# The inverse of the decay blocks kept as two 64x64 blocks per chunk in tiles of 64 columns, and turned two chunks at a time

## The chip, the cores and the metric

The kernel runs on one core of one Trainium2 chip, in float32 where nothing else is said. The metric is the device time of one execution in microseconds, the median of several runs. A core has TensorE (matmuls into PSUM; a transposition, here a "turn", is a matmul with the identity), VectorE, ScalarE and GpSimd (which read and write SBUF, the first two of them PSUM as well), and DMA queues. Each engine works through its own queue in order and waits on semaphores for the others.

## The reference, cut to what matters

Two layers: grouped attention with a mixture of experts behind it, then a gated delta rule with another mixture of experts. Only the gated delta rule is touched. It has 16 key heads, two value heads (units e = 0, 1) to each, 1024 tokens, and is, token by token:

```
S = S * exp(g_t)
kS = k_t . S
S = S + beta_t * k_t (x) (v_t - kS)
o_t = q_t . S
```

The kernel takes it in chunks of 128 tokens. Within a chunk the updates of all tokens come from one triangular system: with U the strictly lower triangular matrix of decayed products k.k times beta, what is wanted is P = (1 + U)^-1 (times beta), 128x128, for 8 chunks and 2 units of each key head.

## The kernel before

The last stage runs a loop over the 16 key heads (lines 1409, 1656, 1801, 2003: one loop on each engine). In each turn of the loop: the decays, k.k and q.k products, the inverse P, and then the scan over 8 chunks, which carries the state S (lines 1515 to 1547). The next head's projection (`project`, L1273), convolution (`conv_op`, L1860, L1862, L1871; written out as a list `todo` from which `more(n)` takes steps) and its copies are laid between the steps of the inverse and the scan, in a fixed order per engine.

The inverse. P is first made for the 16x16 blocks on the diagonal (VectorE, L2023 to L2038, all 16 matrices at once as 128x16 columns). Its last steps spread the blocks to full 128x128 matrices `decay_P` (`e_p`): unit 0 on VectorE (L2042), unit 1 on GpSimd (L1826). TensorE turns these 16 matrices (L1461, four PSUM banks), and ScalarE copies the turned ones to `gmask_Q` (`gm_q`, L1680), so Q = P^T. Then three doublings, level 4 (blocks of 16 to 32), level 5 (32 to 64) and the last (64 to 128). At each of levels 4 and 5, for each unit:

- X = U Q, on 64x64 tiles: low rows (LO, partitions 0 to 63) to low PSUM partitions and high (HI) to high, 16 matmuls of 64 columns (L1476); a float32 matmul is two MATMUL records in the trace, a turn is one
- VectorE takes X through a mask `lmask` into SBUF (L2061, 8 x 64 columns)
- Y = P X, the same tiles (L1486)
- VectorE subtracts Y from half of the columns of Q (L2067)
- TensorE turns Q, 8 matrices of 128x128 per unit, into four banks (L1493), and ScalarE copies them to `decay_P` (L1690).

The last doubling fills one corner of P only: X on one tile (L1500), a copy on 64 partitions (L2071), Y transposed on one tile (L1509), and a copy into the corner of `decay_P` (L1694). Between them stands the first `project_z` (L1321). GpSimd then makes the next head's `gmask_Q` (L1726, 128x2048), which waits for L1500. The scan reads all of `decay_P` (L1533) and begins S with L2094. It waits for both L1694 copies; L1520 is its first matmul that needs S.

In what follows e0 and e1 are the two units. VectorE's order in the doublings is: mask e0, `more(1)`, mask e1, Q e0, Q e1, `more(3)`.

## Time and profile before

| | |
|---|---|
| time, median of 3 runs | 2122.12 us (2114.63 to 2125.47) |
| the profiled execution's own time | 2117.74 us |
| its span | 2115.8 us |
| mean granted clock of TensorE | 0.976 |
| TensorE matmuls busy | 1917.6 us, 91% |
| TensorE weight loads busy | 1402.3 us, 66% |
| VectorE busy | 1505.7 us, 71% |
| ScalarE busy | 984.2 us, 47% |
| GpSimd busy | 759.0 us, 36% |
| DMA, mean | 53 GB/s |

A line number is that of the kernel before. Busy times of different engines overlap, and so do matmuls of one engine; what counts for the time is which engine the others wait for, stage by stage. A timeline row merges instructions of one line: its length runs from the first's start to the last's end, and the last matmul's end lies in the next row's time.

### The profile page before, as it was taken

The page shows a single profiled execution, that of the slowest core. Times are in us where ns is not written, and L with a number is a line of the kernel's source. Part 1 is how long each engine was busy: PE and PEld are TensorE (multiplying, and loading weights), DVE is VectorE, ACT ScalarE, POOL GpSimd, SP SyncE. Part 2 cuts the span into 40 slices and gives each one's busy share as a digit, 9 for nine tenths or more (in the row PEclk, how much of TensorE's full clock was granted, in tenths as well). Part 3 has the DMA queues.
Part 4 walks back from the last instruction along what each step waited for, and adds up shares of the span by engine and source line. Part 5 has one row for each costly group of instructions (what it writes and reads, how often), then busy time and mean ns, then how long its engine had stood idle before and what let it go on. Part 6 is the DMA issues. An engine that isn't in the chain of part 4 may idle for free.

```text
span 2115.8 us, 43478 instructions
## 1 busy us (share of the span) xinstructions
PE 1917.6 (91%) x15082; PEld 1402.3 (66%) x15082; DVE 1505.7 (71%) x2430; ACT 984.2 (47%) x2535; POOL 759.0 (36%) x685
## 2 busy tenths in 40 slices
PE   4578886888799999999999999999999999999998
PEld 3246662333555687877878778787687777877877
DVE  5786771111677687787787877878778787787887
ACT  1012224777213354645545455455564555645544
POOL 4730002110300334616336164362543624526343
PEclk9689998999899999999999999999999999999999
DMA  6635661000122200010010000100001001010010
GB/s 245 209 91 200 184 178 55 26 20 1 55 60 70 82 17 35 5 35 30 15 35 10 30 30 15 35 30 10 30 15 35 30 10 40 5 35 30 15 45 20
DMA packets 75254, 111.75 MB, mean 53 GB/s; under 512 B 23318, under 2 KB 56742, under 8 KB 72006
## 3 DMA queue, kind: packets, MB, share of 16 engines
q1 hardware_dynamic: 71694, 102.32, 15.1%
q0 software_dynamic: 3072, 8.39, 1.3%
q10 hardware_dynamic: 446, 0.48, 0.1%
q8 instruction: 26, 0.43, 0.1%
q14 instruction: 16, 0.13, 0.0%
HBM read 85.80 MB, written 28.52 MB: 54 GB/s over the span
## 4 chain that ended last, share of the span: by engine, by line
PE 51%; DVE 16%; issue 4%; ACT 3%; POOL 0%; DVEq 0%; ACTq 0%; POOLq 0%
PE ps L1273 5%; PE ps L1311 4%; PE ps L1321 4%; DVE conv L1862 3%; DVE P L2034 3%; DVE P_term L2031 3%; PE ps L1544 3%; PE ps L1493 3%; PE ps L1533 3%; PE ps L1428 3%; PE ps L1417 3%; PE ps L1546 3%; PE ps L1520 2%; PE ps L1450 2%; PE ps L1525 2%
## 5 line engine op out<-in xcount | busy, mean ns | idle before, releaser
L1862 DVE SCALAR_TENSOR_TENSOR conv<-raw,tap_st,conv 128x1024 f32<-128x1024 f32 x204 | 299.5, 1468 | 3.6
L1273 PE MATMUL ps<-xnT,w_conv_st 128*128 128x512 f32 x544 | 247.6, 599 | 0.0
L1842 POOL TENSOR_TENSOR o<-o,silu_z 128x256 f32<-128x256 f32 x128 | 138.5, 1082 | 255.5 <-DVE silu_z L1882 141.7
L816 DVE TENSOR_REDUCE m_part<-ps 128x1 f32<-128x640 f32 (+7 forms) x176 | 176.4, 1027 | 67.1 <-PE ps L667 53.5
L1726 POOL TENSOR_TENSOR gmask_Q<-upto,g 128x2048 f32<-128x2048 f32 x17 | 61.4, 3611 | 363.5 <-PE ps L1500 335.5
L998 ACT ACTIVATE probs<-ps 128x1024 f32<-128x1024 f32 (+7 forms) x256 | 145.9, 660 | 58.1 <-PE ps L933 28.7
L1273 PEld LDWEIGHTS ps<-xnT,w_conv_st 128*128 128x128 f32 x544 | 98.9, 191 | 101.1 <-issue 96.2
L1565 ACT COPY raw<-ps 128x512 f32<-128x512 f32 x136 | 80.7, 594 | 173.4 <-PE ps L1273 173.4
L1822 POOL TENSOR_TENSOR kq_decayed<-conv,decay_rows 128x1024 f32<-128x1024 f32 x64 | 159.3, 2521 | 0.0
L1321 PE MATMUL ps<-w_z_st,xnT 128*128 128x256 f32 x512 | 148.8, 393 | 0.0
L903 POOL DMA_INDIRECT slot_outputs<-scratch_slots_y,token_slots x32 | 30.6, 958 | 310.9 <-POOLq L496 202.0
L644 PE MATMUL ps<-k_stack,q_stack 128*128 128x512 bf16 (+3 forms) x384 | 101.6, 357 | 35.8 <-DVE m_part L816 17.8
L1025 DVE COPY oT<-ps 128x1024 f32<-128x1024 f32 x8 | 9.8, 1225 | 171.6 <-PE ps L920 171.6
L933 PE MATMUL ps<-q_stack,k_stack 128*128 x384 | 100.0, 335 | 33.6 <-ACT probs L998 24.4
L1311 PE MATMUL ps<-w_out_st,xn_nat 128*128 128x256 f32 x544 | 126.5, 386 | 3.3 <-ACT xn_nat L1598 2.5
L1311 PEld LDWEIGHTS ps<-w_out_st,xn_nat 128*128 128x128 f32 x544 | 101.8, 192 | 20.3 <-ACT xn_nat L1598 5.7
L1674 ACT ACTIVATE v_nat<-ps,norm_k 128x128 f32<-128x128 f32 x256 | 69.7, 383 | 96.1 <-PE ps L1291 96.1
L933 PEld LDWEIGHTS ps<-q_stack,k_stack 128*128 x384 | 35.9, 98 | 117.4 <-issue 86.8
L1826 POOL TENSOR_TENSOR decay_P<-P,block_mask 128x1024 f32<-128x1024 f32 x16 | 46.0, 2872 | 172.4 <-DVE P L2038 172.4
L2096 DVE SCALAR_TENSOR_TENSOR S<-S,unit_scalars,ps 128x128 f32<-128x128 f32 x192 | 58.1, 344 | 64.7 <-PE ps L1544 64.7
L1698 ACT COPY W<-ps 128x256 f32<-128x256 f32 x128 | 47.7, 373 | 114.6 <-PE ps L1533 112.5
L1571 ACT ACTIVATE tanh_conv<-conv 128x1024 f32<-128x1024 f32 x68 | 71.8, 1055 | 37.0 <-DVE conv L1862 35.0
(345 smaller groups left out, 4728.9 us busy)
## 6 DMA issues: line engine op xcount, KB each, us to landing
decay_rows<-scratch_egc SPq DMA_DIRECT2D x17, 1024.0 KB, 4.7
w_conv_st<-in_w_conv SPq DMA_DIRECT2D x17, 512.0 KB, 3.3
scratch_slots_x<-yacc SPq DMA_DIRECT2D x8, 1024.0 KB, 14.9
slot_rows<-scratch_slots_x SPq DMA_DIRECT2D x16, 512.0 KB, 4.7
scratch_slots_y<-slot_outputs SPq DMA_DIRECT2D x16, 512.0 KB, 3.4
w_gate_up<-in_gu SPq DMA_DIRECT2D x8, 768.0 KB
w_gate_up<-in_gu SPq DMA_DIRECT2D x32, 192.0 KB
kq_decayed<-in_gu SPq DMA_DIRECT2D x22, 256.0 KB, 2.8
```

The costliest lines, as they stand in the source:

```text
L644: return pe.matmul(ps[:, bank, at:at + hi - lo], m.qst[:, REP * i + h, qt * P:(qt + 1) * P], m.kst[:, i, lo:hi], start=first, stop=last)
L816: dve.tensor_reduce(dst, src, AX.X, ALU.max).then_inc(s_max, 1)
L933: mm = pe.matmul(ps[:, b0 + done // HALF, 0:w], m.kst[:, bass.ds(i, 1), kt * P:(kt + 1) * P], m.qst[:, bass.ds(i * REP + h, 1), kt * P + d ...
L998: nc.scalar.activation(pr[:, kt % 2, h, 0:cols], ps[:, 2 * (n % 3):2 * (n % 3) + 2, :].rearrange("p b n -> p (b n)")[:, 0:cols], ACT.Exp, ...
L1273: mm = pe.matmul(ps[:, 6 + n % 2, :], wc[:, k, (n // 2) * P:(n // 2 + 1) * P], m.xnT[:, k, (n % 2) * HALF:(n % 2 + 1) * HALF], start=k == ...
L1311: mm = pe.matmul(ps[:, n, (c % 2) * D:(c % 2 + 1) * D], oT[:, e, c * P:(c + 1) * P], wo[:, e, :], start=e == 0, stop=e == 1)
L1321: mm = pe.matmul(ps[:, 5, 0:256], m.xnT[:, k, c * P:(c + 1) * P], wz[:, k, :], start=k == 0, stop=k == KT - 1)
L1565: nc.scalar.copy(raw[:, n // 2, at:at + HALF], ps[:, 6 + n % 2, :]).then_inc(s_raw, 1)
L1571: nc.scalar.activation(thc[:], cv[:, t, :], ACT.Tanh).then_inc(s_tc, 1)
L1822: g.tensor_tensor(kqe[:, e, a, :], cv[:, a, :], egr[:, e, :], ALU.mult).then_inc(s_kqe, 1)
L1842: g.tensor_tensor(oc, oc, zs[:, c, :], ALU.mult).then_inc(s_oz, 1)
L1862: op = dve.scalar_tensor_tensor(out=cv[:, t, :], in0=raw[:, t, at:at + T], scalar=tap[:, t, at:at + 1], in1=cv[:, t, :], op0=ALU.mult, op1 ...
```

## The change

P and Q of levels 4 and 5 are block diagonal in two 64x64 blocks per chunk. They are now held as 64 columns per chunk instead of 128: `qd` and `pd`, each 128 partitions x 2 units x 8 chunks x 64 columns, both in the room of `gmask_Q`. Consequences:

- The spreads write half (128x512): a mask of half the blocks, `bmask4`.
- All three turns take two chunks at once, [128 x 2*64], so 4 turns per unit instead of 8, into one bank (2 + e). A turn puts chunk 2j on partitions 0 to 63 and chunk 2j+1 on 64 to 127, its low block in columns 0 to 63 and its high block in 64 to 127.
- After the first turn, ScalarE puts the halves back in their places with four copies per unit on 64 partitions (4 chunks x 64 columns each). After the turn of level 4 there is one plain copy (128x512): P stays in the turned layout, and the X and Y matmuls of level 5 take it from there, so that they use all four 64x64 tiles: X goes from rows h to the columns of the chunk's parity, Y back from these rows to h. X and Y there lie in two banks per unit. After the turn of level 5 there are four copies on 64 partitions per unit, straight to the diagonal blocks of `decay_P`.
- X and Y stream 32 columns per block, not 64; VectorE's mask and subtraction are 128x256.
- `lmask` is made for two levels instead of seven; two small reductions of constants are added before the loop.

Core of the diff:

```diff
+        bmask4 = sb("block_mask_of_half", [P, NB // 2])
+        lmask = sb("lmask_of_half", [P, 2, P // 4])
+        xs32 = xs[:, :, 0:NC // 2, :].rearrange("p e c (q n) -> p e (c q) n", q=2)
+        gm_room = gm_q[:].rearrange("p e c n -> p (e c n)")
+        qd = gm_room[:, 0:NC * P].rearrange("p (e c n) -> p e c n", e=2, c=NC)
+        pd = gm_room[:, NC * P:].rearrange("p (e c n) -> p e c n", e=2, c=NC)
+        def place(lv, c, h):
+            j, hi = c // 2, int(h is HI)
+            if lv == FIRST:
+                return h, c, 0, c, 0, c
+            return (LO, HI)[c % 2], 2 * j + hi, hi, j, c % 2, j
+        def halves(e):
+            turned = ps[:, 2 + e, :].rearrange("p (j h n) -> p j h n", h=2, n=64)
+            return [(h, odd, turned[(LO, HI)[odd], :, int(h is HI), :]) for h in (HI, LO) for odd in range(2)]
+        def base(lv, e):
+            return (e, (4, 0)[e], (4, 1)[e])[lv - FIRST]
 tensor:
-                    for c in range(NC):
-                        mm = pe.transpose(ps[:, 2 * e + c // 4, (c % 4) * P:(c % 4 + 1) * P], e_p[:, e, c, :], m.ident[:])
+                    for j in range(NC // 2):
+                        mm = pe.transpose(ps[:, 2 + e, j * P:(j + 1) * P], pd[:, e, 2 * j:2 * j + 2, :].rearrange("p c n -> p (c n)"), m.ident[:])
...
-                                dst = ps[h, e, c * 64:(c + 1) * 64].rearrange("p (b s) -> p b s", s=s)
-                                mm = pe.matmul(dst, ua[h, e, c, 1, h], gm_q[h, e, c, :].rearrange("p (b t s) -> p b t s", t=2, s=s)[:, :, 0, :],
+                                g, at, bank, slot, _, _ = place(lv, c, h)
+                                dst = ps[g, bank + base(lv, e), slot * 32:(slot + 1) * 32].rearrange("p (b s) -> p b s", s=s)
+                                mm = pe.matmul(dst, ua[h, e, c, 1, h], qd[h, e, c, :].rearrange("p (b t s) -> p b t s", t=2, s=s)[:, :, 0, :],
                                                start=True, stop=True)
...
-                                mm = pe.matmul(ps[h, e, c * 64:(c + 1) * 64], e_p[h, e, c, h], xs[h, e, c, :], start=True, stop=True)
+                                g, at, _, _, bank, slot = place(lv, c, h)
+                                mm = pe.matmul(ps[h, bank + base(lv, e), slot * 32:(slot + 1) * 32], pd[g, e, at, :], xs32[g, e, at, :], start=True, stop=True)
...
-                        for c in range(NC):
-                            mm = pe.transpose(ps[:, 2 + 2 * e + c // 4, (c % 4) * P:(c % 4 + 1) * P], gm_q[:, e, c, :], m.ident[:])
+                        for j in range(NC // 2):
+                            mm = pe.transpose(ps[:, 2 + e, j * P:(j + 1) * P], qd[:, e, 2 * j:2 * j + 2, :].rearrange("p c n -> p (c n)"), m.ident[:])
 scalar:
-                    nc.scalar.copy(chunks(gm_q[:, e]), two_banks(2 * e)).then_inc(s_q, 1)
+                    for h, odd, src in halves(e):
+                        last = nc.scalar.copy(qd[h, e, odd::2, :], src)
+                    last.then_inc(s_q, 1)
...
-                    nc.scalar.copy(chunks(e_p[:, e]), two_banks(2 + 2 * e)).then_inc(s_pt, 1)
+                    if lv == FIRST:
+                        nc.scalar.copy(chunks(pd[:, e]), ps[:, 2 + e, :]).then_inc(s_pt, 1)
+                    else:
+                        for h, odd, src in halves(e):
+                            last = nc.scalar.copy(e_p[h, e, odd::2, h], src)
+                        last.then_inc(s_pt, 1)
 gpsimd and vector (spread; the same on pc[:, 0:NC] for unit 0):
-                g.tensor_tensor(e_p[:, 1].rearrange("p c (b i) -> p c b i", i=BLK),
-                                pc[:, NC:, :].unsqueeze(2).broadcast_to([P, NC, NB, BLK]),
-                                bmask[:].unsqueeze(1).unsqueeze(3).broadcast_to([P, NC, NB, BLK]), ALU.mult).then_inc(s_p1, 1)
+                g.tensor_tensor(pd[:, 1].rearrange("p c (b i) -> p c b i", i=BLK),
+                                pc[:, NC:, :].unsqueeze(2).broadcast_to([P, NC, NB // 2, BLK]),
+                                bmask4[:].unsqueeze(1).unsqueeze(3).broadcast_to([P, NC, NB // 2, BLK]), ALU.mult).then_inc(s_p1, 1)
 vector:
-                        mask = m.lmask[:, lv, :].unsqueeze(1).broadcast_to([P, NC, 64])
-                        dve.tensor_tensor(xs[:, e], ps[:, e, :].rearrange("p (c n) -> p c n", c=NC), mask, ALU.mult).then_inc(s_xt, 1)
+                        mask = lmask[:, lv - FIRST, :].unsqueeze(1).broadcast_to([P, NC, 32])
+                        if lv == FIRST:
+                            made, taken = ps[:, e, 0:NC * 32].rearrange("p (c n) -> p c n", c=NC), xs32[:, e]
...
+                        dve.tensor_tensor(taken, made, mask, ALU.mult).then_inc(s_xt, 1)
...
-                        dst = gm_q[:, e, :, :].rearrange("p c (b t s) -> p c b t s", t=2, s=s)[:, :, :, 0, :]
-                        dve.tensor_tensor(dst, dst, ps[:, e, :].rearrange("p (c b s) -> p c b s", c=NC, s=s), ALU.subtract).then_inc(s_yt, 1)
+                            dst = qd[:, e].rearrange("p c (b t s) -> p c b t s", t=2, s=s)[:, :, :, 0, :]
+                            made = ps[:, e, 0:NC * 32].rearrange("p (c b s) -> p c b s", c=NC, s=s)
...
+                        dve.tensor_tensor(dst, dst, made, ALU.subtract).then_inc(s_yt, 1)
```

## Rows read from the trace of the kernel before

**Rows 1.** The page: the chain that ended last, its share of the span by engine.
```profile
PE 51%; DVE 16%; issue 4%; ACT 3%; POOL 0%; DVEq 0%; ACTq 0%; POOLq 0%
```

**Rows 2.** Windows, one turn of the head loop: busy time (instructions) per engine, granted clock.
```profile
1368.50:1455.40 86.90, 83.63 (x722) 66.50 (x720) 70.36 (x118) 46.23 (x132) 38.56 (x32) 1.00 0.07 24
```

**Rows 3.** Source view, line 2042 (duration min/median/max, first and last start).
```profile
L2042 DVE TENSOR_TENSOR decay_P<-P,block_mask x16: 1224/1224/1224, 738.4 to 2041.6; 128x1024 f32<-128x1024 f32 x16
```

**Rows 4.** Timeline of TensorE, one head: start, us, line, tiles, matmuls, idle time before.
```profile
1426.18 8.75 PE L1273 MATMUL ps<-xnT,w_conv_st 128*128 128x512 f32 x20
1435.05 1.09 PE L1461 MATMUL ps<-ident,decay_P 128*128 128x128 f32 x8
...
1440.38 2.08 PE L1476 MATMUL ps<-gmask_Q,att_U 64*64 64x64 f32 x64
1442.42 1.15 PE L1486 MATMUL ps<-X,decay_P 64*64 64x64 f32 x32
1443.89 1.15 PE L1486 MATMUL ps<-X,decay_P 64*64 64x64 f32 x32 [0.33 <-DVE X L2061]
1444.97 1.98 PE L1273 MATMUL ps<-xnT,w_conv_st 128*128 128x512 f32 x4
1446.79 1.91 PE L1493 MATMUL ps<-ident,gmask_Q 128*128 128x128 f32 x16
1448.63 2.08 PE L1476 MATMUL ps<-gmask_Q,att_U 64*64 64x64 f32 x64
...
1452.46 1.15 PE L1486 MATMUL ps<-X,decay_P 64*64 64x64 f32 x32 [0.65 <-DVE X L2061]
...
1455.43 2.08 PE L1500 MATMUL ps<-gmask_Q,att_U 64*64 64x64 f32 x32
...
1458.50 2.08 PE L1509 MATMUL ps<-decay_P,X 64*64 64x64 f32 x32
...
1461.43 0.61 PE L1533 MATMUL ps<-v_nat,decay_P 128*128 128x128 f32 x4
...
1463.97 0.71 PE L1520 MATMUL ps<-S,kq_decayed 128*128 128x128 f32 x4 [0.17 <-DVE S L2094]
```

**Rows 5.** Timeline of VectorE, the same stretch.
```profile
1434.91 2.42 DVE L1860 TENSOR_SCALAR conv<-raw,tap_st 128x1024 f32<-128x1024 f32 x1
...
1441.58 0.69 DVE L2061 TENSOR_TENSOR X<-ps,lmask 128x512 f32<-128x512 f32 x1 [0.29 <-PE ps L1476]
1442.19 0.74 DVE L1860 TENSOR_SCALAR conv<-raw,tap_st 128x1024 f32<-128x1024 f32 x1
...
1445.08 0.69 DVE L2067 TENSOR_TENSOR gmask_Q<-gmask_Q,ps 128x512 f32<-128x512 f32 x1 [0.74 <-PE ps L1486]
...
1446.82 2.60 DVE L1862 SCALAR_TENSOR_TENSOR conv<-raw,tap_st,conv 128x1024 f32<-128x1024 f32 x2
...
1457.57 1.30 DVE L2071 COPY X<-ps 64x512 f32<-64x512 f32 x2
...
1459.44 4.28 DVE L1862 SCALAR_TENSOR_TENSOR conv<-raw,tap_st,conv 128x1024 f32<-128x1024 f32 x2
...
1464.37 0.41 DVE L1882 SCALAR_TENSOR_TENSOR silu_z<-tanh_z,ps 128x256 f32<-128x256 f32 x1
```

**Rows 6.** Source view, line 446 (both shapes, first and last start).
```profile
L446 PE MATMUL ps<-w_attn_sb,xnT x64: 248/276/323, 37.1 to 44.1; 128*128 128x64 f32 x32, 128*128 128x32 f32 x32
```

**Rows 7.** Windows, line 920 alone: busy us (matmuls).
```profile
335.60:337.70 2.10, 1.92 (x16) 0.42 (x16) 1.00 0.41 111
```

**Rows 8.** Timeline of GpSimd, the same stretch.
```profile
1433.91 2.87 POOL L1826 TENSOR_TENSOR decay_P<-P,block_mask 128x1024 f32<-128x1024 f32 x1 [10.56 <-DVE P L2038]
1457.71 3.61 POOL L1726 TENSOR_TENSOR gmask_Q<-upto,g 128x2048 f32<-128x2048 f32 x1 [20.93 <-PE ps L1500]
```

**Rows 9.** Groups by line and shape, ScalarE (busy us, mean ns, idle before).
```profile
L1698 ACT COPY W<-ps 128x256 f32<-128x256 f32 x128 | 47.7, 373 | 114.6 <-PE ps L1533 112.5
...
L1680 ACT COPY gmask_Q<-ps 128x1024 f32<-128x1024 f32 x32 | 32.4, 1012 | 13.0 <-PE ps L1461 13.0
```

More of the change, by code:

```diff
@@ L165, in build @@
         m.future = sb("future", [P, P], BF16)
-        m.lmask = sb("lmask", [P, LEVELS, P // 2])
+        m.lmask = sb("lmask", [P, 2, P // 2])
         m.minus_half = sb("minus_half", [P, 1])
@@ L619, in _ @@
             step.link(g.memset(m.lmask[:], 1.0))
-            for lv in range(LEVELS):
-                s = 1 << lv
-                ap = m.lmask[:, lv, :].rearrange("p (b s) -> p b s", s=s)
+            for n in range(2):
+                s = 1 << (FIRST + n)
+                ap = m.lmask[:, n, :].rearrange("p (b s) -> p b s", s=s)
                 step.link(g.affine_select(out=ap, in_=ap, compare_op=ALU.is_ge, fill=0.0, base=-s,
@@ L1499, in _ @@
                     for c in range(NC):
-                        mm = pe.matmul(ps[HI, e, c * 64:(c + 1) * 64], ua[LO, e, c, 1, HI], gm_q[LO, e, c, LO], start=True, stop=True)
+                        mm = pe.matmul(ps[HI, base(LEVELS - 1, e), c * 64:(c + 1) * 64], ua[LO, e, c, 1, HI], qd[LO, e, c, :], start=True, stop=True)
                     mm.then_inc(s_x, 1)
@@ L1508, in _ @@
                     for c in range(NC):
-                        mm = pe.matmul(ps[LO, e, c * 64:(c + 1) * 64], xs[HI, e, c, :], e_p[HI, e, c, HI], start=True, stop=True)
+                        mm = pe.matmul(ps[LO, base(LEVELS - 1, e), c * 64:(c + 1) * 64], xs[HI, e, c, :], e_p[HI, e, c, HI], start=True, stop=True)
                     mm.then_inc(s_y, 1)
@@ L1693, in _ @@
                     act.wait_ge(s_y, i * ND + NT + e + 1)
-                    nc.scalar.activation(e_p[LO, e, :, HI], ps[LO, e, :].rearrange("p (c n) -> p c n", c=NC), ACT.Copy,
+                    nc.scalar.activation(e_p[LO, e, :, HI], ps[LO, base(LEVELS - 1, e), :].rearrange("p (c n) -> p c n", c=NC), ACT.Copy,
                                          scale=-1.0).then_inc(s_pt, 1)
@@ L1798, in _ @@
             g.tensor_copy(tap[:], m.taps[:, 1]).then_inc(s_taps, 1)
-            pool.wait_ge(s_dve, 5)
+            pool.wait_ge(s_dve, 7)
             passed()
@@ L1991, in _ @@
                     step(dve.tensor_reduce(hmask[:], bmask[:].rearrange("p (q t) -> p t q", t=2), AX.X, ALU.add))
+                    step(dve.tensor_reduce(bmask4[:], bmask[:].rearrange("p (h b) -> p b h", h=2), AX.X, ALU.add))
+                    step(dve.tensor_tensor(lmask[:], m.lmask[:, :, 0:P // 4], m.lmask[:, :, P // 4:], ALU.add))
                     step.wait()
@@ L2041, in _ @@
                 dve.wait_ge(s_ch, i * SUBS + n)
-                dve.tensor_tensor(e_p[:, 0].rearrange("p c (b i) -> p c b i", i=BLK),
-                                  pc[:, 0:NC, :].unsqueeze(2).broadcast_to([P, NC, NB, BLK]),
-                                  bmask[:].unsqueeze(1).unsqueeze(3).broadcast_to([P, NC, NB, BLK]), ALU.mult).then_inc(s_p0, 1)
+                dve.tensor_tensor(pd[:, 0].rearrange("p c (b i) -> p c b i", i=BLK),
+                                  pc[:, 0:NC, :].unsqueeze(2).broadcast_to([P, NC, NB // 2, BLK]),
+                                  bmask4[:].unsqueeze(1).unsqueeze(3).broadcast_to([P, NC, NB // 2, BLK]), ALU.mult).then_inc(s_p0, 1)
                 todo = ([(0, k) for k in range(TAPS)] + [(1, 0), (0, TAPS)] + [(1, k) for k in range(1, TAPS)]
@@ L2059, in _ @@
                         dve.wait_ge(s_x, i * ND + n0 + e + 1)
-                        mask = m.lmask[:, lv, :].unsqueeze(1).broadcast_to([P, NC, 64])
-                        dve.tensor_tensor(xs[:, e], ps[:, e, :].rearrange("p (c n) -> p c n", c=NC), mask, ALU.mult).then_inc(s_xt, 1)
+                        mask = lmask[:, lv - FIRST, :].unsqueeze(1).broadcast_to([P, NC, 32])
+                        if lv == FIRST:
+                            made, taken = ps[:, e, 0:NC * 32].rearrange("p (c n) -> p c n", c=NC), xs32[:, e]
+                        else:
+                            made = ps[:, base(lv, e):base(lv, e) + 2, 0:NC * 16].rearrange("p b (j n) -> p b j n", n=32)
+                            taken = xs32[:, e].rearrange("p (j b) n -> p b j n", b=2)
+                            mask = lmask[:, lv - FIRST, :].unsqueeze(1).unsqueeze(1).broadcast_to([P, 2, NC // 2, 32])
+                        dve.tensor_tensor(taken, made, mask, ALU.mult).then_inc(s_xt, 1)
                         if e == 0:
@@ L2065, in _ @@
                         dve.wait_ge(s_y, i * ND + n0 + e + 1)
-                        dst = gm_q[:, e, :, :].rearrange("p c (b t s) -> p c b t s", t=2, s=s)[:, :, :, 0, :]
-                        dve.tensor_tensor(dst, dst, ps[:, e, :].rearrange("p (c b s) -> p c b s", c=NC, s=s), ALU.subtract).then_inc(s_yt, 1)
+                        if lv == FIRST:
+                            dst = qd[:, e].rearrange("p c (b t s) -> p c b t s", t=2, s=s)[:, :, :, 0, :]
+                            made = ps[:, e, 0:NC * 32].rearrange("p (c b s) -> p c b s", c=NC, s=s)
+                        else:
+                            dst = qd[:, e, :, 0:s].rearrange("p (j b) n -> p b j n", b=2)
+                            made = ps[:, base(lv, e):base(lv, e) + 2, 0:NC * 16].rearrange("p b (j n) -> p b j n", n=s)
+                        dve.tensor_tensor(dst, dst, made, ALU.subtract).then_inc(s_yt, 1)
                     more(3)
@@ L2070, in _ @@
                     dve.wait_ge(s_x, i * ND + NT + e + 1)
-                    dve.tensor_copy(xs[HI, e], ps[HI, e, :].rearrange("p (c n) -> p c n", c=NC)).then_inc(s_xt, 1)
+                    dve.tensor_copy(xs[HI, e], ps[HI, base(LEVELS - 1, e), :].rearrange("p (c n) -> p c n", c=NC)).then_inc(s_xt, 1)
                 silu_z(i, 0)
@@ L2114, in mix_out @@
                 dve.tensor_tensor(y[:, pair], y[:, pair], mixed[n % 2], ALU.add).then_inc(s_mixed, 1)
-            step.n = 5
+            step.n = 7
             early, late = slice(0, NC // 2), slice(NC // 2, NC)
```

## The prediction, on record before the changed kernel ran

> **What bounds the kernel now.** The page first: the chain that ended last runs over TensorE for 51% of the span, over VectorE for 16% and over ScalarE for 3% [rows 1]. Then one turn of the loop over the 16 key heads, between equal points of two turns: TensorE works 83.6 of 86.9 us at a granted clock of 1.00, VectorE 70.4, ScalarE 46.2, GpSimd 38.6 [rows 2]. The spread of P opens the part that is changed; its 16 starts lie from 738.4 to 2041.6 us, so a turn takes 1303.2 / 15 = 86.9 us [rows 3], and what one turn gains counts 16 times. Last, the timelines of one turn. The reader is to see in TensorE's [rows 4] that the doublings (1435.05 to 1461.43) are nearly gapless: only 0.33 us of idle time on VectorE before a Y at level 4, 0.65 us in the same place at level 5. So matmul time taken out there is won, until VectorE's queue comes up behind it; VectorE carries convolution steps between the pieces of the inverse [rows 5].
>
> **Turns.** 8 matmuls fewer in the first turn and 8 in each of the two others, 24 per key head. 16 of them take 1446.79 to 1448.63, 0.115 us each [rows 4]: 0.92 us for 8, 2.76 us in all, all on TensorE's path.
>
> **X and Y of levels 4 and 5.** They stream 32 columns, not 64, with the same 64-column weights. Would that be faster? Line 446 holds 32 matmuls of 64 and 32 of 32 columns with 128-column weights; its 64 starts go from 37.1 to 44.1, 0.111 us each whatever the columns, against 0.115 us for 128 columns above [rows 4, 6]. So with 128-column weights the weights set the pace below 128 columns. For 64-column weights the nearest row is the last X, one tile at a time with 64 columns: 32 in 2.01 us, 63 ns each, about half of 0.115 [rows 4]. I read that as the pace of the weights too and take no gain from the narrower stream. The lower bound of the cost is half.
>
> **Tiles of level 5.** Level 4 keeps its two tiles (low rows to low columns, high to high), which run side by side: 64 in 2.04 us, 32 ns each, half of the 63 ns of one tile [rows 4]. At level 5 all four tiles are used in turn. Line 920 tells that column tiles on the same rows overlap: 16 matmuls of 512 columns in 1.92 us, where one 512-column matmul of a projection takes 1.82 / 4 = 0.46 [rows 4, 7]. So four tiles will not be slower than two; whether they are faster is left open. I take 32 ns, with 15 (four side by side) and 63 (one at a time) as bounds.
>
> In the Trainium skill, "TensorE: Matmul & The Clock Gate", section "The mechanism", weight loads overlap running matmuls only between different row groups; the new Y of level 5 uses each row group twice in a row and would suffer. The trace disagrees: the last X stays in one row group and still issues every 63 ns. By the rule, Y would fall back to about one tile at a time, which the third rival below prices from rows.
>
> **VectorE.** The 128x512 operations on X and Q (0.69) become 128x256 (0.41, the silu_z row) [rows 5]: 0.28 less, eight times, of which only those ahead of a waiting Y or turn count. The spread of P falls from 1.22 to 0.69. GpSimd's own spread took 2.87 and ended at 1436.78; the convolution step that began at 1434.91 ended at 1437.33, right behind it, against 0.75 for such a step unhindered (1442.19, between two X masks) [rows 5, 8]. Half the elements end GpSimd's at about 1435.4, so VectorE's chain of four steps is through near 1440.0, not 1441.3, just before X needs it.
>
> **ScalarE.** The first copy (128x1024, 1.01) becomes four of 64x256. A 128x256 copy is 0.37 [rows 9], so four take at most 1.5; as copies in a row overlap somewhat, I take 1.2 for four and 2.3 for eight, against 1.9 for the two long copies. The level-4 copy falls to 0.59; the level-5 ones grow to 2.3 for both. Cover: in the first turn the projections (1.8 each) lie above it; behind level 5, 2.0 us of last X. With 1.5 for four the first X would still wait for TensorE alone, and L1509 would come 0.2 later. Without the cover the cost would be about 0.4 us per head and turn.
>
> **The sum, piece by piece.** Up to the first X: TensorE ends its fifth projection near 1434.8 (the row ends at 1434.93, and the next line's matmuls begin about 0.15 before a row's end, as 1446.79 does before 1446.95) and waits until 1435.05 for VectorE's spread [rows 4]; that 0.25 goes, and 0.92 of turns. First X at 1439.2, not 1440.38: 1.17 us won. ScalarE's last copy ends near 1438.8 and does not hold it.
> From the first X (now 0), before and after [rows 4, 5]: Y of the second head starts at 3.51, after at 2.98 (VectorE's mask is 0.3 shorter, then TensorE itself is the limit). Projection 1.82 and 8 turns: X of level 5 at 8.25, after 6.83. Here VectorE takes over: behind the second Q of level 4 it has three convolution steps (1445.08 to 1449.42 with that Q, so 3.7 for the steps). That Q now begins at 4.15 (Y at 2.98, 0.93 of matmuls, 0.24 until VectorE starts) and takes 0.35, so VectorE reaches the level-5 mask at 8.25, though X is ready at 8.05. Then mask 0.4, one convolution step 1.2, mask 0.4: second Y at 12.08, after 10.32. Turns: last X at 15.05, after 12.55; the second turn waits 0.2 for VectorE's Q. Then VectorE again: Q at 11.5 (10.32 + 0.93 + 0.24), then three steps (1.2 + 0.75 + 1.3), so the copy of X begins at 15.15 (17.19 before), and L1509 at 16.0 instead of 18.12. The scan begins at 18.93 instead of 21.05.
> One more late thing: the first S of the scan. gmask (3.61) starts behind the last X and ended at 1461.32; the two convolution steps begun at 1459.44 took 4.28 instead of 2.6 and ended at 1463.72, 2.4 behind gmask, and S came behind them, so L1520 waited 0.17 [rows 4, 5, 8]. After: gmask from 14.8 or 15.15 (a convolution step is running at its start) to 18.4 to 18.8, S's copies from 20.8 to 21.1 on. TensorE would be there at 21.3. L1520 at 23.59, after about 21.4: 2.2 won.
> In "SBUF — State Buffer", section "Who interferes with whom", the Trainium skill has a VectorE instruction with two SBUF inputs and a GpSimd one that reads SBUF exclude each other, whoever starts first; the two rows above agree, and by it gmask starts at 15.15. The sum is the same for either start.
> In all 1.17 + 2.18 = 3.35 us per head, 53.6 for 16. Of 5.2 us (2.8 of turns, 2.2 of VectorE's eight operations, 0.25) that is two thirds; the rest is swallowed where VectorE's queue sets the pace. Behind L1520 scan, outputs and the next head are unchanged and shift as a whole. The two more constants of VectorE and ten fewer mask instructions of GpSimd lie before the loop, under 0.5 us. The profiled execution took 2117.7 us (span 2115.8 and 1.9 around it), 4.4 below the median of the runs shown; 2117.7 - 53.6 = 2064, by the median 2068.5. I forecast 2066, halfway, and count the rivals from the same base (2119.6).
>
> **Rivals.**
> 1. Four tiles overlap, or the narrow streams count. If level 5 goes at 15 ns, X there is hidden by VectorE, and only the last Y shortens (0.47): 3.8 us per head, 2059. If level 4 goes so too, X, Y and VectorE's whole queue move up: replayed, 4.8 us, 2043. For: line 920. Against: line 446 has the weights as the pace. 0.22 together (0.07 for 2043).
> 2. Small waits that I left out (semaphores between more instructions, drains where tile shapes change, 0.14 behind each Y today): 0.3 to 1 us per head, 2071 to 2082. 0.17.
> 3. Row neighbours of Y at level 5 don't overlap: 64 matmuls at up to 63 ns; the first is partly under the mask wait, the second adds 0.9, about 1.35 in all: 2.0 us per head, 2088. Against: [rows 7]. 0.04.
> 4. No change to speak of: all of level 5 one tile at a time. 128 matmuls times 31 ns is 4 us, 0.8 of it under VectorE: 3.2 lost against 3.35 won: 2117. 0.03.
> 5. Slower: as 4, and every change of tile drains. From matmuls of one shape to another the path pays 0.14 (second Y of level 4, 0.93 of work, begins 1443.89; the projection 1444.97) [rows 4]. At 64 changes times 0.05 to 0.14 us: 3 to 9 us per head, 2165 to 2260. It decides from 3.35 / 64 = 52 ns per change with 2 or more tiles, or from 2 ns if the tiles don't overlap either. Against: line 920 changes its tile at each matmul without such a cost. 0.04.
> The forecast itself has 0.50, its own range 2060 to 2071.
>
> **Range and chances.** Leaving out 2043 below and the serial cases above, 2046 to 2084 holds a good 8 in 10. A measurement of this kernel (2114.6 to 2125.5) tells about 0.5%, 10.6 us, from no change. Faster: all but rivals 4 and 5, 0.93; same 0.03; slower 0.04.
>
> **What would show it.** Right: a turn of 83.5 us; L1493 with 256 matmuls, L1461 with 128; L1476 and L1486 with 32 columns and still 2.04 us per 64 at level 4; idle time of TensorE behind VectorE's X at level 5 grown from 0.65 to between 0.5 and 1; the POOL spread under 1.6; L1520 waiting little for S. Wrong: level 4's 64 matmuls in about 1 us (rival 1), level 5's at 4 us (rivals 4, 5), TensorE idle behind a ScalarE copy before the first X, or a clock below 1.00 in the loop.

## The result, and the profile after

The changed kernel takes 2143.63 us (median of 5 runs, 2136.76 to 2147.95), the kernel before 2122.12 on the same chip: 1.010 times the time before, 95% interval 1.008 to 1.013. So it is slower by 1%, where 2066 and a gain were forecast. The profiled execution took 2139.09 us, span 2137.2. (The runs further on were made on several chips, on which the kernel before takes 2087, 2084 and 2122 us; each is compared with the kernel before on its own chip, with a 95% interval in brackets.) A ratio leaves out runs that took over 1.5% longer than the fastest run of the same kernel, which concerns fill_narrow alone.

From the page of the kernel after: the span, the busy times, the granted clock in 40 slices, and the chain that ended last by engine.

```profile
span 2137.2 us, 42854 instructions
PE 1918.4 (90%) x14658; PEld 1407.5 (66%) x14698; DVE 1441.4 (67%) x2432; ACT 998.5 (47%) x2727; POOL 731.9 (34%) x675
...
PEclk9699998999799989989889898899988989889998
...
PE 58%; DVE 8%; ACT 6%; issue 2%; POOL 0%; DVEq 0%; ACTq 0%; POOLq 0%
```

The same clock line of the kernel before:

```profile
PEclk9689998999899999999999999999999999999999
```

The head loop fills the slices from about the 14th on. Before, every slice there was a 9; after, there are 8s all through the loop. VectorE's share of the chain fell from 16% to 8% and TensorE's rose from 51% to 58% [rows 1].

Windows of the kernel after, each one head (from one spread of P to the next); columns as in [rows 2]: length, busy time of PE, PEld, DVE, ACT and POOL, granted clock, DMA share, GB/s.

```profile
831.00:914.30 83.30, 78.85 (x698) 62.04 (x697) 66.38 (x117) 47.07 (x143) 37.13 (x33) 1.00 0.07 25
914.30:1003.10 88.80, 84.82 (x698) 67.54 (x697) 66.15 (x117) 47.07 (x143) 37.12 (x33) 0.92 0.06 24
...
1358.30:1448.80 90.50, 86.51 (x698) 68.95 (x697) 66.27 (x117) 47.05 (x143) 37.17 (x33) 0.91 0.07 23
```

These are the same 698 records with three lengths. Three of the 15 head windows look like the first, about 83.35 us; twelve have a clock below 1.00. Nine of those take about 88.8 us, two 90.5, and the loop's first 91.5. Before, a head took 86.9 at 1.00 [rows 2, 3]. Now one fallen head next to an undisturbed one, cut at the points where their work is the same: from the first X to the end of the last Y of level 5, then up to the scan.

```profile
836.50:847.40 10.90, 9.09 (x268) 7.65 (x268) 8.60 (x13) 4.04 (x6) 0.00 (x0) 1.00 0.15 48
847.40:856.40 9.00, 8.50 (x99) 7.43 (x93) 8.33 (x9) 4.89 (x13) 3.67 (x1) 1.00 0.00 0
919.80:930.70 10.90, 9.09 (x268) 7.68 (x268) 8.65 (x13) 4.04 (x6) 0.00 (x0) 1.00 0.13 48
930.70:944.40 13.70, 13.70 (x98) 12.26 (x92) 8.53 (x9) 4.56 (x12) 3.61 (x1) 0.50 0.00 0
```

The doublings are equal to the tenth. Right behind them the granted clock is 0.50, 1.2 instead of 2.4 GHz, for 13.7 us, and about a hundred records (98 and 99) take 13.7 us, not 9.0. It is so in each of the twelve: the clock is 1.00 in the first 15 us of the head and 0.50 to 0.52 from 16.7 to 30 us. The windows hold less TensorE work than they look: 9.09 us busy in 10.9.

TensorE's timeline of the undisturbed head, from the first X to the scan (start, us, line, tiles, records, idle time before):

```profile
836.42 2.06 PE L1500 MATMUL ps<-gmask_Q,att_U 64*64 64x32 f32 x64 [0.19 <-ACT gmask_Q L1706]
838.28 2.20 PE L1511 MATMUL ps<-X,gmask_Q 64*64 64x32 f32 x64
...
843.20 1.14 PE L1500 MATMUL ps<-gmask_Q,att_U 64*64 64x32 f32 x64
845.29 0.67 PE L1511 MATMUL ps<-X,gmask_Q 64*64 64x32 f32 x32 [0.95 <-DVE X L2101]
846.82 0.67 PE L1511 MATMUL ps<-X,gmask_Q 64*64 64x32 f32 x32 [0.86 <-DVE X L2101]
847.42 1.26 PE L1518 MATMUL ps<-ident,gmask_Q 128*128 128x128 f32 x8
848.61 2.08 PE L1525 MATMUL ps<-gmask_Q,att_U 64*64 64x64 f32 x32
851.18 1.13 PE L1344 MATMUL ps<-w_z_st,xnT 128*128 128x256 f32 x4 [0.50 <-ACT decay_P L1721]
852.24 2.08 PE L1534 MATMUL ps<-decay_P,X 64*64 64x64 f32 x32
...
855.18 0.61 PE L1558 MATMUL ps<-v_nat,decay_P 128*128 128x128 f32 x4
...
857.38 0.61 PE L1545 MATMUL ps<-S,kq_decayed 128*128 128x128 f32 x4
```

And of the fallen head, the part behind its second Y of level 5:

```profile
930.76 1.97 PE L1518 MATMUL ps<-ident,gmask_Q 128*128 128x128 f32 x8
932.66 3.67 PE L1525 MATMUL ps<-gmask_Q,att_U 64*64 64x64 f32 x32
...
938.26 3.67 PE L1534 MATMUL ps<-decay_P,X 64*64 64x64 f32 x32
...
943.63 0.96 PE L1558 MATMUL ps<-v_nat,decay_P 128*128 128x128 f32 x4
```

From the turn behind the last Y of level 5 to the scan it is 7.76 us in the one (847.42 to 855.18) and 12.87 in the other (930.76 to 943.63). No wait stands behind that: each line has the same records, each taking 1.6 to 1.8 times as long. These 5.1 us and 0.35 more in the first rows of the scan are the 5.5 that the head is longer.

ScalarE's copies of the halves, undisturbed head (the second row is all eight of level 5):

```profile
834.78 1.50 ACT L1706 COPY gmask_Q<-ps 64x256 f32<-64x256 f32 x4
...
848.11 3.02 ACT L1721 COPY decay_P<-ps 64x256 f32<-64x256 f32 x8 [0.68 <-PE ps L1518]
```

**The account.** Fifteen heads now take 1321.7 us, before 1303.2 [rows 3]. Without falls they would take about 1251.1, which is what the run fill_first below shows (mean 83.4; the loop's first head is 0.9 longer in it). So 52.1 us are won, and 70.6 given back in twelve heads, 5.9 each. The 16th head falls too (2.0 us over its time before), and 0.9 is lost ahead of the loop: 18.5 + 2.0 + 0.9 = 21.4, the whole difference of the spans, 2137.2 against 2115.8.

### The profile page after: what moved, and what is told of

The parts are those of the page before. It is cut to its first block, busy times and chain, and to the rows that moved or that the text cites. A ratio compares the mean times of both kernels' runs of the same rounds, so it can differ in the third digit from the quotient of the medians.

```text
span 2137.2 us, 42854 instructions
## 1 busy us (share of the span) xinstructions
PE 1918.4 (90%) x14658; PEld 1407.5 (66%) x14698; DVE 1441.4 (67%) x2432; ACT 998.5 (47%) x2727; POOL 731.9 (34%) x675
## 4 chain that ended last, share of the span: by engine, by line
PE 58%; DVE 8%; ACT 6%; issue 2%; POOL 0%; DVEq 0%; ACTq 0%; POOLq 0%
PE ps L1296 7%; PE ps L1344 5%; PE ps L1334 4%; PE ps L1473 3%; PE ps L1569 3%; PE ps L1558 3%; PE ps L1571 3%; DVE conv L1894 3%; PE ps L1440 3%; PE ps L1451 3%; PE ps L1534 2%; PE ps L1545 2%; ACT gmask_Q L1706 2%; PE ps L1525 2%; PE ps L1511 2%
## 5 line engine op out<-in xcount | busy, mean ns | idle before, releaser
L1894 DVE SCALAR_TENSOR_TENSOR conv<-raw,tap_st,conv 128x1024 f32<-128x1024 f32 x204 | 285.8, 1401 | 3.6
L1344 PE MATMUL ps<-w_z_st,xnT 128*128 128x256 f32 x512 | 165.3, 429 | 1.5 <-ACT decay_P L1721 1.5
L644 PE MATMUL ps<-k_stack,q_stack 128*128 128x512 bf16 (+3 forms) x360 | 94.7, 350 | 41.9 <-DVE m_part L816 21.1
L1344 PEld LDWEIGHTS ps<-w_z_st,xnT 128*128 128x128 f32 x512 | 90.3, 207 | 14.5 <-ACT decay_P L1721 1.9
```

Of the source, the lines that this page charges most:

```text
L644: return pe.matmul(ps[:, bank, at:at + hi - lo], m.qst[:, REP * i + h, qt * P:(qt + 1) * P], m.kst[:, i, lo:hi], start=first, stop=last)
L1344: mm = pe.matmul(ps[:, 5, 0:256], m.xnT[:, k, c * P:(c + 1) * P], wz[:, k, :], start=k == 0, stop=k == KT - 1)
L1894: op = dve.scalar_tensor_tensor(out=cv[:, t, :], in0=raw[:, t, at:at + T], scalar=tap[:, t, at:at + 1], in1=cv[:, t, :], op0=ALU.mult, op1 ...
```

## The experiments

The theory: the change does what was worked out, but TensorE has less to do in the doublings, and its clock falls behind them. The rival explanations: the fall comes from something else in the heads (other work, another execution), the four tiles do it, or the new tiles and copies cost time themselves. "Falls" are head windows with a granted clock below 1.00, out of 15, in the profiled execution; the head times are in us. The last three kernels leave products or turns out, as told at each, and are there for their times alone.

| kernel | ratio to before | falls | head, undisturbed | head, fallen |
|---|---|---|---|---|
| after | 1.010 [1.008, 1.013] | 12 | 83.35 | 88.8, 90.5 |
| after_again | 1.010 [1.007, 1.013] | 12 | 83.4 | 88.8, 90.5 |
| fill_gaps | 0.974 [0.971, 0.976] | 0 | 83.5 | |
| fill_first | 0.974 [0.972, 0.977] | 0 | 83.35 | |
| fill_no_wait | 0.974 [0.972, 0.975] | 0 | 83.3 | |
| turn_twice | 0.977 [0.974, 0.981] | 0 | 83.9 | |
| fill_narrow | 0.986 [0.981, 0.990] | 10 | 83.4 | 88.8, 90.5 |
| fill_elsewhere | 1.004 [1.002, 1.006] | 4 | 85.7 | 91.3 |
| wide_x | 1.006 [1.005, 1.008] | 11 | 83.4 | 88.9, 90.5 |
| two_tiles | 1.014 [1.011, 1.018] | 13 | 83.6 | 89.1, 90.7 |
| before_half_turns | 0.995 [0.993, 0.997] | 0 | 86.2 | |
| before_narrow4 | 1.008 [1.006, 1.010] | 8 | 86.8 | 88.5, 90.0 |
| before_narrow | 1.013 [1.007, 1.019] | 15 | | 88.3, 90.0 |

### fill_gaps: a matmul in each of the two waits of level 5

One matmul of 128x512 whose result nobody reads (two records), ahead of each wait for X at level 5. All else is the changed kernel.

```diff
 for e in range(2):
+    if lv > FIRST:
+        pe.wait_ge(s_raw, (i + 1) * 8 + 7)
+        for _ in range(1):
+            pe.matmul(ps[:, 6, :], m.ident[:], m.xnT[:, 0, 0:HALF], start=True, stop=True)
     pe.wait_ge(s_xt, i * ND + n0 + e + 1)
```

> The changed kernel, with one 128x512 matmul (identity on xnT, result thrown away, a PSUM bank nobody reads) ahead of each of the two waits for X at level 5, where TensorE was idle for 0.95 and 0.86 us. The clock theory (TensorE does too little in the doublings and is set to 1.2 GHz behind them) expects the clock to stay at 1.00 in all or most heads, a head of 83.4 to 84 us and about 2066 us in all. The rival (the fall belongs to the new form of levels 4 and 5, not to the idle time) expects heads of 88.8 us as now and 2140 to 2150 us.

Measured: 2032.08 against 2086.98, ratio 0.974. A head window, and TensorE's timeline at level 5:

```profile
790.50:874.00 83.50, 80.84 (x702) 62.59 (x701) 66.40 (x117) 47.09 (x144) 37.20 (x32) 1.00 0.07 25
```

```profile
803.09 1.14 PE L1500 MATMUL ps<-gmask_Q,att_U 64*64 64x32 f32 x64
804.15 1.13 PE L1507 MATMUL ps<-xnT,ident 128*128 128x512 f32 x2
805.21 0.67 PE L1515 MATMUL ps<-X,gmask_Q 64*64 64x32 f32 x32
805.81 1.12 PE L1507 MATMUL ps<-xnT,ident 128*128 128x512 f32 x2
806.86 0.67 PE L1515 MATMUL ps<-X,gmask_Q 64*64 64x32 f32 x32
```

The filler takes 1.06 us, about what the wait was (0.95 and 0.86), so the doublings end 0.15 later. All 15 heads are at 1.00. Two matmuls per head that compute nothing take the ratio from 1.010 to 0.974: the fall is the whole loss, and the rest of the change is worth 54.9 us. (0.974 of 2122.12 is 2066, as expected.)

### wide_x: X streams 64 columns again

X of levels 4 and 5 takes all 64 columns of Q, and VectorE picks the 32 that count.

```diff
-dst = ps[g, bank + base(lv, e), slot * 32:(slot + 1) * 32].rearrange("p (b s) -> p b s", s=s)
-mm = pe.matmul(dst, ua[h, e, c, 1, h], qd[h, e, c, :].rearrange("p (b t s) -> p b t s", t=2, s=s)[:, :, 0, :],
+mm = pe.matmul(ps[g, bank + base(lv, e), slot * 64:(slot + 1) * 64], ua[h, e, c, 1, h], qd[h, e, c, :],
                start=True, stop=True)
```

> The changed kernel with X of levels 4 and 5 streaming all 64 columns again instead of 32; the mask takes the 32 it needs. If 64-column weights set the pace, the time of X at level 4 stays at 2.04 us per 64 matmuls and TensorE moves twice the columns in it. Theory one (narrow streams at level 4 lower the activity) expects fewer falls of the clock, 2070 to 2110 us. Theory two (the idle time and four tiles at level 5 do it) expects 13 falls of 16 as now, 2140 us.

Measured: 2100.2, ratio 1.006. X at level 4 and at level 5:

```profile
1406.98 2.08 PE L1499 MATMUL ps<-gmask_Q,att_U 64*64 64x64 f32 x64 [0.20 <-ACT gmask_Q L1705]
...
1413.79 1.16 PE L1499 MATMUL ps<-gmask_Q,att_U 64*64 64x64 f32 x64
```

Twice the columns take the same time, 1.89 (to the first Y) against 1.86 for level 4 and 1.16 against 1.14 for level 5: the narrow stream wins nothing on TensorE. Eleven heads of 15 fall, one of them only to 0.98 (84.4 us). So the columns of X alone don't restore the clock.

### two_tiles: level 5 on two tiles at a time

```diff
-for c in range(NC):
+for c in (range(NC) if lv == FIRST else (0, 2, 4, 6, 1, 3, 5, 7)):
```

(for X and for Y; even chunks use two of the four tiles, odd chunks the other two)

> The changed kernel with level 5 in another order, all even chunks and then all odd ones, so that only two of the four tiles can run side by side. X and Y of level 5 should go back from about 1.1 to 2.0 us per 64 matmuls, in the place of the idle time; a head grows by the last Y alone, 0.5 us, 83.9. If idle time of TensorE at level 5 brings the clock down, it stays up now: about 2075 us. If the columns moved count and not the time in which something runs, nothing is gained: 2140 to 2155 us.

Measured: 2117.61, ratio 1.014.

```profile
1428.90 1.46 PE L1500 MATMUL ps<-gmask_Q,att_U 64*64 64x32 f32 x64
1430.99 0.92 PE L1511 MATMUL ps<-X,gmask_Q 64*64 64x32 f32 x32 [0.63 <-DVE X L2101]
1432.52 0.92 PE L1511 MATMUL ps<-X,gmask_Q 64*64 64x32 f32 x32 [0.60 <-DVE X L2101]
```

Less overlap (0.92 for a Y, not 0.67) fills part of the waits: 0.63 and 0.60 of idle time, not 0.95 and 0.86. Yet 13 heads fall. So the fall doesn't need four tiles at once, and a third less idle time doesn't help when it is narrow matmuls that fill it. The expectation of 2.0 us for 64 matmuls was too high: X took 1.46. For a Y both tiles have the same rows, and its 32 records still take 0.85 us (1432.52 to 1433.37), 27 ns each, against 63 for one tile.

### turn_twice: the turns of levels 4 and 5 made twice

```diff
-for j in range(NC // 2):
+for j in (*range(NC // 2), *range(NC // 2)):
```

> The changed kernel with every turn of levels 4 and 5 made twice in a row (8 matmuls per unit as before the change, the second set writing the same values). Costs TensorE 1.84 us per head, some of it under VectorE. The clock theory expects a clock at 1.00 and a head of 84.7 to 85.2 us, 2087 to 2096 us in all. If the taken-out turns have no part in it, 88.8 + 1.8 us per head, 2170 us.

Measured: 2039.02, ratio 0.977, no fall in 15 heads.

```profile
789.50:873.40 83.90, 80.43 (x714) 63.88 (x713) 66.57 (x117) 47.31 (x144) 37.14 (x32) 1.00 0.07 25
```

```profile
1475.42 0.67 PE L1511 MATMUL ps<-X,gmask_Q 64*64 64x32 f32 x32 [0.17 <-DVE X L2101]
1476.95 0.67 PE L1511 MATMUL ps<-X,gmask_Q 64*64 64x32 f32 x32 [0.86 <-DVE X L2101]
```

16 more turns a head (x714) cost 0.5 us of it and save the clock. They put back as many turns as the change had removed there. But they don't leave the waits as they were: the doubled turns of level 4 lie ahead of X, and the first wait of level 5 shrinks from 0.95 to 0.17, while the second stays at 0.86. So this run doesn't tell whether it is the turns themselves that help or the shorter wait. It does show that the second wait need not be filled.

### after_again, fill_narrow, fill_elsewhere, before_narrow

after_again is the changed kernel once more, beside the other three.

> The changed kernel itself, as a mark for the chip and the day. Both theories: 1.01 times the kernel before, heads of 83.35 us without and 88.8 to 90.5 with a fall of the clock, 12 to 14 falls in 16 heads.

Measured: 2105.7 against 2083.74, ratio 1.010, 12 falls. The falls are no accident of one execution or of one chip.

fill_narrow fills the two waits with eight matmuls of 64x64 weights and 32 columns, all on one tile:

```diff
+    if lv > FIRST:
+        pe.wait_ge(s_raw, (i + 1) * 8 + 7)
+        pe.sem_inc(s_passed, 1)
+        for _ in range(8):
+            pe.matmul(ps[LO, 6, 0:32], m.ident[LO, LO], m.xnT[LO, 0, 0:32], start=True, stop=True)
```

> As fill_gaps, but each gap is filled with 8 matmuls of 64x64 weights and 32 columns on one tile instead of one of 128x512: about the same time (16 records of 58 ns, 0.93 us), a small part of the array and few columns. If it counts that TensorE has something running, the clock stays up and the ratio to the kernel before is 0.974 again. If it counts how much of the array is moved, 12 to 14 falls and a ratio of about 1.01.

Measured: four runs of 2048.19, 2057.97, 2086.66 and 2094.74, with a mean granted clock of 0.973, 0.966, 0.952 and 0.947 (after_again on the same chip: 0.941). The ratio 0.986 is of the first two; the median of all four, 2072.32, is 0.994. The profile is of the run of 2086.66:

```profile
1319.02 1.09 PE L1508 MATMUL ps<-xnT,ident 64*64 64x32 f32 x16
1320.15 0.67 PE L1516 MATMUL ps<-X,gmask_Q 64*64 64x32 f32 x32
1320.61 1.09 PE L1508 MATMUL ps<-xnT,ident 64*64 64x32 f32 x16
1321.68 0.83 PE L1516 MATMUL ps<-X,gmask_Q 64*64 64x32 f32 x32
1322.44 1.97 PE L1523 MATMUL ps<-ident,gmask_Q 128*128 128x128 f32 x8
```

TensorE is busy without a gap through level 5, and the clock is at 1.2 GHz from the second Y on all the same (the turns behind it take 1.97, in an undisturbed head 1.26). Having TensorE busy in both waits is not enough, then: eight small matmuls take as long as one of 512 columns, and 10 heads fell in this execution. By their times and clocks the two shorter runs had fewer: above 0.974 of the kernel before, at 5.9 us a fall, the four times make about 3, 5, 10 and 11 falls (an estimate, from these times and the 70.6 us in twelve heads). One kernel can fall often in one execution and seldom in the next.

fill_elsewhere puts the two wide fillers ahead of the k.k products, a dense place:

```diff
 pe.wait_ge(s_acc, i * 16 + 16)
+for _ in range(2):
+    pe.matmul(ps[:, 6, :], m.ident[:], m.xnT[:, 0, 0:HALF], start=True, stop=True)
```

> The two filling matmuls of fill_gaps, but at the start of each head, ahead of the products of k with k, where TensorE is dense anyway; there they cost their full 1.75 us. If the place counts (the thin stretch of the doublings), 12 to 14 falls stay and a head takes 90.6 us on average or so, a ratio of 1.02 to 1.03. If only the work per head counts, the clock stays up: 85.1 us per head, a ratio of 0.985.

Measured: 2091.35, ratio 1.004.

```profile
792.50:883.80 91.30, 86.72 (x701) 68.23 (x700) 65.23 (x117) 46.83 (x143) 36.91 (x32) 0.93 0.07 23
883.80:969.50 85.70, 80.63 (x701) 62.81 (x700) 65.60 (x117) 46.81 (x143) 36.99 (x33) 1.00 0.08 24
```

An undisturbed head is 2.3 us longer, a little more than the two fillers (2.1). The falls go from 12 to 4, not to 0 and not 12 again. It fits neither "any extra work helps" nor "only work at the thin place helps"; the length of a head, which this edit changes too, may decide how often the fall is hit. That was not taken apart.

before_narrow is the kernel before with 32-column streams for X and Y of levels 4 and 5, its tiles and turns as they were. It leaves out the products of the other 32 columns, and VectorE takes what older products left in their place:

```diff
-dst = ps[h, e, c * 64:(c + 1) * 64].rearrange("p (b s) -> p b s", s=s)
-mm = pe.matmul(dst, ua[h, e, c, 1, h], gm_q[h, e, c, :].rearrange("p (b t s) -> p b t s", t=2, s=s)[:, :, 0, :],
+at = c * 64 + 32 * int(h is HI)
+dst = ps[h, e, at:at + 32].rearrange("p (b s) -> p b s", s=s)
+mm = pe.matmul(dst, ua[h, e, c, 1, h], gm_q[h, e, c, h].rearrange("p (b t s) -> p b t s", t=2, s=s)[:, :, 0, :],
...
-mm = pe.matmul(ps[h, e, c * 64:(c + 1) * 64], e_p[h, e, c, h], xs[h, e, c, :], start=True, stop=True)
+at = 32 * int(h is HI)
+mm = pe.matmul(ps[h, e, c * 64 + at:c * 64 + at + 32], e_p[h, e, c, h], xs[h, e, c, at:at + 32], start=True, stop=True)
```

> The kernel before with X and Y of levels 4 and 5 streaming 32 columns instead of 64 (the half on each block's own diagonal; VectorE still takes 64, so what stands in the other half of Q is left over from older products). Nothing else is changed. If 64-column weights set the pace, a head takes 86.8 us as before. If the narrow stream alone were enough to bring the clock down, 5 us per head more, a ratio of 1.03 to 1.04; I expect 0 to 4 falls, since the turns are all there, and a ratio of 1.00 to 1.01.

Measured: 2113.47, ratio 1.013.

```profile
895.24 3.78 PE L1273 MATMUL ps<-xnT,w_conv_st 128*128 128x512 f32 x4
...
1423.13 2.06 PE L1477 MATMUL ps<-gmask_Q,att_U 64*64 64x32 f32 x64
...
1426.61 1.12 PE L1488 MATMUL ps<-X,decay_P 64*64 64x32 f32 x32 [0.35 <-DVE X L2063]
...
1429.48 1.91 PE L1495 MATMUL ps<-ident,gmask_Q 128*128 128x128 f32 x16
...
1435.12 1.12 PE L1488 MATMUL ps<-X,decay_P 64*64 64x32 f32 x32 [0.67 <-DVE X L2063]
1436.18 3.63 PE L1495 MATMUL ps<-ident,gmask_Q 128*128 128x128 f32 x16
```

This is the cleanest of the runs. Times and waits of the doublings are those of [rows 4] (X 2.06 against 2.08, Y 1.12 against 1.15, idle 0.35 and 0.67 against 0.33 and 0.65), only the streams are narrower, and every one of the 15 heads falls, where 0 to 4 were expected. Eleven fall behind the Ys of level 5: the turns of 1436.18 take 3.63, those of 1429.48 took 1.91. The four heads of 90.0 us fall behind the Ys of level 4 already: the projection of 895.24 takes 3.78, in [rows 4] 1.98. The falls are short here, and a head costs 88.3 or 90.0 in place of 86.9. The narrow streams make the kernel 1.3% slower. (The values differ too, since half of them are left over from older products. That isn't taken apart here; before_half_turns below also works on left-over values and falls nowhere.)

### fill_first, fill_no_wait, before_half_turns, before_narrow4

fill_first keeps only the first of the two fillers (`if lv > FIRST and e == 0`).

> fill_gaps with the first of the two filling matmuls alone (half the dose). The density theory (what counts is how thin TensorE's work is over the stretch of level 4 and 5 as a whole) expects fewer falls than 13, between 0 and 6 of 16, a ratio of 0.974 to 0.99. If both gaps must be closed, 12 to 14 falls and 1.01.

Measured: 2068.93 against 2121.86, ratio 0.974, no falls, 83.35 a head. One matmul of 512 columns is enough. It fills the first wait; the second, 0.82 us in this run, stays.

fill_no_wait is fill_gaps without the wait ahead of the first `project_z`, for ScalarE's last copy of P. (Each last Y keeps its own wait for the copy that it reads.)

```diff
-pe.wait_ge(s_pt, i * ND + NT)
 project_z(i, 0)
```

> fill_gaps without the wait of project_z for ScalarE's level-5 copies, which the changed kernel's own banks no longer need and for which TensorE stood 0.5 us in each head. The clock stays at 1.00; a head of 83.0 to 83.3 us instead of 83.53, a ratio to the kernel before of 0.968 to 0.973. If VectorE's copy of X is what holds the next matmuls, nothing is gained: 0.974.

Measured: 2065.59, ratio 0.974, a head of 83.3 for 83.5.

```profile
848.33 2.05 PE L1537 MATMUL ps<-decay_P,X 64*64 64x64 f32 x32 [0.31 <-DVE X L2119]
```

The 0.50 of ScalarE's copies is gone, but 0.31 comes back one instruction later behind VectorE's copy of X. Too small to show in the ratio.

before_half_turns is the kernel before with only the even chunks turned at levels 4 and 5 (`for c in range(0, NC, 2)`); for the odd chunks an older P is left.

> The kernel before with only the even chunks turned at levels 4 and 5 (4 matmuls per unit instead of 8; the odd chunks of P are left over). X and Y keep 64 columns. A head is 1.4 to 1.8 us shorter if the clock holds, 85.0 to 85.4, a ratio of 0.98. If fewer turns alone make the stretch thin enough, falls of the clock take that back: a ratio of 1.00 to 1.03. From before_narrow I expect the narrow streams to be the greater part and 0 to 3 falls here.

Measured: 2111.13, ratio 0.995, no falls, 86.2 a head (86.9 before).

```profile
1361.12 1.15 PE L1486 MATMUL ps<-X,decay_P 64*64 64x64 f32 x32 [0.54 <-DVE X L2061]
```

16 turns less are 1.84 us of TensorE [rows 4], of which 0.7 is won. The rest goes into new waits for VectorE, 0.54 ahead of the first Y of level 5, 0.20 in the turns behind it and 0.30 ahead of L1509. With half of the turns, and with waits of 0.54 and 0.65 at level 5, but with 64-column streams, no head falls. So neither fewer turns nor waits of that length bring the clock down by themselves.

before_narrow4 is before_narrow with the narrow streams at level 4 only.

> before_narrow with the narrow streams at level 4 alone, which stands between two projections; level 5 streams 64 columns as before (the halves of Q off the diagonal are left over). If it is the length of the thin stretch that counts, no or few falls and a ratio of 1.000. If narrow streams anywhere bring the clock down, falls in most heads and a ratio of 1.01 as in before_narrow.

Measured: 2137.16, ratio 1.008, 8 falls of 15.

The projection behind the Ys of level 4, in a head that falls (88.5 us) and in the next one, which doesn't (86.8):

```profile
840.20 3.49 PE L1273 MATMUL ps<-xnT,w_conv_st 128*128 128x512 f32 x4
...
928.67 1.98 PE L1273 MATMUL ps<-xnT,w_conv_st 128*128 128x512 f32 x4
```

All eight falls are there, behind level 4, and none behind level 5, where the streams are 64 columns wide again. So the fall comes behind narrow streams: behind level 4 here, behind level 4 or level 5 in before_narrow, which has them at both. There is no sharp step between "holds" and "falls" over the heads of one kernel; this one falls in some of them.

## Why the prediction was wrong

**The step that failed** is the one that the whole sum rests on: "TensorE works 83.6 of 86.9 us at a granted clock of 1.00", read from the kernel before and carried over to the kernel after without a term for it. The only trace of doubt was half a line at the end, "or a clock below 1.00 in the loop"; no rival and no chance stood for it. The runs show about 76 us given back: 70.6 in twelve heads and 5.5 in the 16th (2.0 over its time before and the 3.5 that it should have won). The same work with one more matmul a head (fill_first) is 2.6% faster than before.

**The sum itself held.** An undisturbed head is 83.35 us, 83.5 was forecast; 3.53 won for 3.35. fill_gaps won 54.9 us, 53.6 was forecast. That it is so close is in part luck: ahead of the first X 0.27 less was won than forecast, behind it 0.45 more. By its parts, from the first X of [rows 4] and of the timeline after:

| from the first X | forecast | measured |
|---|---|---|
| first X itself, won | 1.17 | 0.90 |
| X of level 5 | 6.83 | 6.78 |
| second Y of level 5 | 10.32 | 10.40 |
| last X | 12.55 | 12.19 |
| last Y (L1509, now L1534) | 16.0 | 15.82 |
| L1520 (now L1545) | 21.4 | 20.96 |

(0.90 is what is left of 3.53 behind the 23.59 - 20.96 = 2.63 won from the first X on.)

- **Turns**: right. 8 records, not 16, in 1.0 us.
- **Narrow streams**: right that they win no time. Level 4 takes 1.86 us for 64 at 32 columns, 1.89 at 64 (wide_x), 2.04 before. The second half of rival 1, 2043, is out. What the text didn't see is that they cost something: by before_narrow they are enough to bring the clock down in every head.
- **Tiles of level 5**: 32 ns was taken, the bounds were 15 and 63. Measured: 64 records in 1.14 us with four tiles, 18 ns; with two tiles at a time 1.46 (two_tiles). The first half of rival 1 came true, and with it the shorter second Y of level 5: 0.60 (846.82 to 847.42), not 0.93, which is most of the 0.44 by which L1520 is early. Of rival 2 only the small waits for ScalarE below are seen. Rivals 3, 4 and 5 are out; so is the rule of the Trainium skill weighed against the trace ("TensorE: Matmul & The Clock Gate", section "The mechanism"), by which Y would have gone back to one tile at a time.
- **VectorE**: right. Idle time ahead of Y at level 5 was forecast to grow to between 0.5 and 1; it is 0.95 and 0.86 [rows 4: 0.65]. Its share of the chain halved.
- **ScalarE**: mis-sized. Four copies take 1.50, the bound, not 1.2, so TensorE waits 0.19 ahead of the first X; eight take 3.02, not 2.3, and TensorE waits 0.50 behind the last X. "The first X would still wait for TensorE alone" was wrong by that 0.19; the 0.50 was hidden in good part by VectorE's copy, which fill_no_wait shows as the next wait.
- **GpSimd and S**: right. The spread takes 1.45 (under 1.6), and L1545 no longer waits for S.

**Why the clock falls.** Shown: in the changed kernel the fall comes at the same place in each fallen head, right behind the doublings; in the kernel before, narrow streams bring it (before_narrow), and it comes behind the level that has them (all eight falls of before_narrow4 behind level 4); taking out half of the turns doesn't (before_half_turns); in the changed kernel, with both and four tiles, putting back either the turns (turn_twice) or 1.06 us of wide matmul (fill_first) removes it in all heads; narrower filling of the same time doesn't do it reliably (two_tiles, fill_narrow), nor do wider streams for X alone (wide_x). So a row that the profile counts as busy does not always keep the clock up. In the Trainium skill, "TensorE: Matmul & The Clock Gate" tells in the section "A second HAM failure mode: psum-queue depth-cycling" that frequent micro-idles between groups of matmuls make the clock oscillate. The changed kernel agrees as far as it goes (its two waits of 0.9 us, falls in 12 of 15 heads), but two runs go beyond it: before_narrow has 0.04 us more idle time in the doublings than the kernel before and 15 falls of 15, and fill_narrow fell in 10 heads with both waits filled.

Open: what decides which head falls (12, 11, 13, 10, 8 or 4 of 15 of nearly equal heads); why a fall costs 5.5 us or more in the changed kernel and 1.5 or 3.1 in before_narrow; whether turns help as such, since turn_twice also shortens a wait; and how far off work may stand and still help (fill_elsewhere). Y alone wide again was not run on the changed kernel, nor X and Y together.

**The version to keep** is fill_first (or fill_gaps): 0.974 of the time before [0.972, 0.977], 0.964 of the changed kernel's (0.9742 / 1.0102).

## What to carry to other kernels

When an edit takes matmul work out of a dense stretch, or makes streams narrower, the clock is a term of the sum: give it a rival with a price (in the changed kernel 5.5 to 7 us for each fall, up to 16 times), and look at the granted clock head by head, not at the mean. Where a narrower stream wins no time, as here (1.14 us against 1.16 for 64 records), leave it wide unless someone else gains by it: in before_narrow it cost 1.3%. And where TensorE waits anyway, a wide matmul into a PSUM bank that nobody reads is a cheap trial: here one of 1.06 us for each head turned +1.0% into -2.6%. Run it several times: the four runs of fill_narrow lay 2.3% apart.
